# Attention of batch 0 starts once batch 0 is split; batch 1 is split by GpSimd inside the head loop; k and v from a folded weight

## The reference, cut to what matters

```
k, v = x @ Wk, x @ Wv;   q = x @ Wq
latent = (k + v) @ W_down_kv          # 32 features
k_rec, v_rec = latent @ W_up_k, latent @ W_up_v
scores = q . k_rec * scale            # per head, clipped
scores *= exp(-1e-4 * |i - j|)
out = softmax(scores) @ v_rec
```

## Time and profile before

| | us |
|---|---|
| median of 3 runs | 1162.07 (1161.68 to 1163.52) |
| the profiled execution | 1161.56, span 1159.8 |
| first scores of attention | at 91.75 |
| TensorE busy | 1048.4 (90%) |
| VectorE busy | 854.3 (74%) |
| ScalarE busy | 819.0 (71%) |
| GpSimd busy | 226.8 (20%) |

### The profile page before, as it was taken

One profiled execution on the slowest core, in us unless ns is written; L12 is line 12 of the kernel. 1 busy time (PEld: TensorE's weight loads), 2 busy tenths in 40 slices (PEclk: granted clock), 3 DMA queues, 4 the chain that ended last, 5 costly groups with the idle time before them and its releaser, 6 DMA issues.

```text
span 1159.8 us, 20386 instructions
## 1 busy us (share of the span) xinstructions
PE 1048.4 (90%) x5228; PEld 690.5 (60%) x5260; DVE 854.3 (74%) x1998; ACT 819.0 (71%) x1339; POOL 226.8 (20%) x316
## 2 busy tenths in 40 slices
PE   4637999999999659999999999999998998899997
PEld 2212322223222427888888888888885776777876
DVE  5953344433444587999999999999997787688897
ACT  5447999999999346887787788788775443266665
POOL 7553444454445200000000000000004112000000
PEclk9768999999999889999999999999999999699999
DMA  3454666666666217666776766666641000043231
GB/s 98 118 155 147 219 208 196 209 216 214 198 202 210 71 35 292 245 247 231 244 248 232 241 250 232 239 251 233 236 171 55 1 1 1 3 137 120 87 109 37
DMA packets 92918, 192.54 MB, mean 166 GB/s; under 512 B 9676, under 2 KB 56396, under 8 KB 82636
## 3 DMA queue, kind: packets, MB, share of 16 engines
q1 hardware_dynamic: 92884, 192.15, 49.1%
HBM read 154.03 MB, written 38.08 MB: 166 GB/s over the span
## 4 chain that ended last, share of the span: by engine, by line
PE 79%; DVE 9%; issue 4%; ACT 3%; POOL 2%; DMA 2%; ACTq 0%; DVEq 0%; SPq 0%; POOLq 0%
PE bank L1163 25%; PE bank L1176 15%; PE bank L1033 10%; PE bank L1170 8%; PE bank L1015 6%; PE bank L1018 5%; ACT ring L811 2%; PE bank L1265 1%; PE bank L1044 1%; DVE xn L1356 1%; DVE ring L1406 1%; POOL m_norm L722 1%; PE bank L1249 1%; DMA ring<-c_rows 1%; DVE stats L1344 1%
## 5 line engine op out<-in xcount | busy, mean ns | idle before, releaser
L811 ACT ACTIVATE ring<-bank,minus_bound 128x1024 f32<-128x1024 f32 x256 | 271.1, 1110 | 30.5 <-DVE bank L1439 13.6
L1163 PE MATMUL bank<-xh,w_parts 128*128 128x512 f32 x896 | 277.3, 391 | 1.8 <-DVEq L1564 1.8
L867 ACT ACTIVATE bank<-bank 128x512 f32<-128x512 f32 x320 | 186.2, 582 | 91.0 <-PE bank L1163 91.0
L1578 DVE TENSOR_TENSOR bank<-bank,ring 128x512 f32<-128x512 f32 x320 | 223.7, 699 | 29.8 <-DMA ring<-c_rows 6.6
L1176 PE MATMUL bank<-hh,w_parts 128*128 128x512 f32 x776 | 239.8, 390 | 0.0
L1570 DVE TENSOR_TENSOR hl<-bank,hh 128x512 fp32r<-128x512 f32 x321 | 218.2, 680 | 0.1
L1439 DVE TENSOR_TENSOR bank<-bank,corner 128x128 f32<-128x128 f32 x256 | 76.4, 299 | 173.7 <-PE bank L1018 145.1
L861 ACT ACTIVATE hh<-bank 128x512 fp32r<-128x512 f32 x321 | 190.4, 593 | 3.1 <-DVE bank L1578 3.0
L1163 PEld LDWEIGHTS bank<-xh,w_parts 128*128 128x128 f32 x896 | 168.0, 188 | 38.0 <-DVEq L1564 2.3
L1163 PE MATMUL bank<-xl,w_parts 128*128 128x512 f32 x448 | 174.7, 390 | 0.0
L1176 PEld LDWEIGHTS bank<-hh,w_parts 128*128 128x128 f32 x776 | 145.9, 188 | 30.6 <-ACT hh L861 0.4
(11 more groups left out here) (259 smaller groups left out, 1193.0 us busy)
## 6 DMA issues: line engine op xcount, KB each, us to landing
ring<-c_rows SPq DMA_DIRECT2D x80, 1024.0 KB, 5.1
w_parts<-w_pairs SPq DMA_DIRECT2D x160, 128.0 KB, 2.5
w_pairs<-xh SPq DMA_DIRECT2D x16, 768.0 KB, 4.4
q_stack<-q_parts SPq DMA_DIRECT2D x64, 144.0 KB
k_stack<-k_parts SPq DMA_DIRECT2D x64, 144.0 KB
w_pairs<-xl SPq DMA_DIRECT2D x16, 512.0 KB, 3.5
ring<-c_rows SPq DMA_DIRECT2D x16, 512.0 KB, 4.5
big<-in_w_exp SPq DMA_DIRECT2D x16, 384.0 KB, 4.8
```

What stands on the lines that cost most here:

```text
L811: act.activation(ring[:, c % RING * S:(c % RING + 1) * S], wide[c % 2][:], ACT.Exp, bias=minus_bound[:]).then_inc(exp_done, 1)
L867: act.activation(bank(4 + c % ZB), bank(4 + c % ZB), ACT.Silu).then_inc(silu_ready, 1)
L1163: ins = pe.matmul(out_, w[i], x_[j], start=start and k == 0, stop=stop and k == 2, skip_group_check=not start)
L1578: dve.tensor_tensor(bank(4 + c % ZB), bank(4 + c % ZB), cb[u][:, g * GW:(g + 1) * GW], ALU.mult).then_inc(hid_ready, 1)
```

## The change

- k and v come from one folded weight a_up = (Wk + Wv) W_down W_up, made at the start by three small products with a ScalarE copy behind each. TensorE then needs one product of xnT for k and one per tile for v; it forms them between the transposes of later groups. ScalarE's order is written out by hand.
- VectorE and GpSimd split groups 0 and 1 only. Third parts are written by the last subtraction straight as bf16, so a third cast falls away on both. `folded`, `parts` and `qk_f` have a buffer for each group that needs one.
- q is stored as three rows, and loaded threefold; k is stored by one DMA of three parts (384 KB). A group takes 8 DMAs where it took 16. Heads 0 and 1 are loaded behind the stores of group 1.
- Groups 2 and 3 are eight late parts (two variants of q and of k each). GpSimd makes part 0 before the head loop and part i+1 in turn i, by itself, casts included; SyncE stores it at the end of the turn. Seven turns are written out; then SyncE waits for all late stores and the loop goes on.
- The squares of all groups are reduced by VectorE behind its two splits, with three banks instead of two.
- `decay` and `unfold` are computed only in the slow branch; `corner` comes from 128 columns; its reciprocal is taken between bound and flag, and the flag is set before the correction and `minus_bound`.
- VectorE fills the eight stack buffers with zeros at its start. GpSimd zeroes `hh` and `hl` by four copies at the start of the head loop. The fills of `evac[1]` and `ring` are gone; GpSimd's other early fills stand before the first normalisation.

The diff, cut to its core (blank lines left out):

```diff
...
+        parts = [ring[:, u * 3 * S:(u + 1) * 3 * S].bitcast(BF16).rearrange("p (s i t) -> p s i t", s=4, i=3) for u in range(2)]
+        qk_f = [t.rearrange("p (w t) -> p w t", w=2)
+                for t in (ring[:, 6 * S:7 * S], ring[:, 7 * S:8 * S], big[:, 0:S], big[:, S:2 * S])]
+        late_size = 3 * GW // 2
+        late_homes = [(big, 5 * S + k * late_size) for k in range(4)] + [(xnT, k * late_size) for k in range(2)]
+        late_parts = [t[:, at:at + late_size] for t, at in late_homes]
+        late_parts += [xn[:, :, :].rearrange("p t d -> p (t d)")[:, k * late_size:(k + 1) * late_size] for k in range(2)]
+        late_parts = [t.bitcast(BF16).rearrange("p (i t) -> p i t", i=3) for t in late_parts]
...
-        q_dram = [dram(f"q_parts{s}", [NH, 5, HD, S], BF16) for s in range(2)]
-        k_dram = [dram(f"k_parts{s}", [NH, 3, HD, S], BF16) for s in range(2)]
+        q_dram = [dram(f"q_parts{s}", [NH, 3, HD, S], BF16) for s in range(2)]
+        k_dram = [dram(f"k_parts{s}", [NH, HD, 3, S], BF16) for s in range(2)]
...
-            for g in range(G):
-                b, o = g // 2, (g % 2) * GW
-                if g == 2:
-                    sp.wait_ge(parts_saved[0], 16 * 16)
-                    sp.wait_ge(parts_saved[1], 16 * 16)
-                    sp.wait_ge(stacks_zero, 1)
-                    load_stacks(0, 0)
-                    load_stacks(1, 1)
-                sp.wait_ge(parts_ready, g + 1)
-                for w, drams in ((0, q_dram), (2, k_dram)):
-                    if w == 2:
-                        sp.wait_ge(part_cast, 6 * (g + 1))
-                    for v in range(2):
-                        rows = drams[v][b * H:(b + 1) * H]
-                        for i in range(rows.shape[1]):
-                            sp.dma_start(rows[:, i, :, o:o + GW], parts[g % 2][:, w + v, i % 3, :]).then_inc(parts_saved[g % 2], 16)
-            for u in range(2):
-                sp.wait_ge(parts_saved[u], 2 * 16 * 16)
+            def store_part(g, s_, part, saved):
+                at = (q_dram, k_dram)[s_ // 2][s_ % 2][g // 2 * H:(g // 2 + 1) * H, :, :, g % 2 * GW:(g % 2 + 1) * GW]
+                if s_ < 2:
+                    for i in range(3):
+                        sp.dma_start(at[:, i, :, :], part[:, i, :]).then_inc(saved, 16)
+                else:
+                    sp.dma_start(at.rearrange("h d i t -> (h d) i t"), part).then_inc(saved, 16)
+            for g in range(2):
+                for s_ in range(4):
+                    if s_ == 0:
+                        sp.wait_ge(parts_ready, g + 1)
+                    if s_ >= 2:
+                        sp.wait_ge(folded_ready, 6 * g + 4 + s_ - 1)
+                    store_part(g, s_, parts[g][:, s_, :, :], parts_saved)
+            sp.wait_ge(parts_saved, 2 * 8 * 16)
+            sp.wait_ge(stacks_zero, 1)
+            load_stacks(0, 0)
+            load_stacks(1, 1)
+            def store_late(k):
+                sp.wait_ge(late_ready, k + 1)
+                store_part(2 + k // 4, k % 4, late_parts[k], late_saved)
...
-                with sp.Fori(0, NH // 2 - 1) as i:
+                for i in range(7):
+                    next_heads(i, whole)
+                    if i == 0:
+                        store_late(0)
+                    store_late(i + 1)
+                sp.wait_ge(late_saved, 2 * 8 * 16)
+                with sp.Fori(7, NH // 2 - 1) as i:
...
-            for u in range(2):
-                for v in range(2):
-                    link.sign(pool.memset(q_stack[v][u][:], 0.0))
-                    link.sign(pool.memset(k_stack[v][u][:], 0.0))
...
-            link.sign(pool.memset(evac[1][:], 1.0))
-            link.sign(pool.memset(ring[:, 6 * S:8 * S], 0.0))
-            link.wait()
-            pool.sem_inc(stacks_zero, 1)
-            pool.wait_ge(table, 5)
...
+            pool.wait_ge(folds_ready, 1)
+            for g in range(2):
                 pool.wait_ge(k_ready, g + 1)
+                if g:
+                    pool.wait_ge(xnT_ready, G)
                 for w in range(2):
...
+                    pool.tensor_tensor(folded[g][2 + w], qk_f[g][:, 1, :], fold[:, w, g * GW:(g + 1) * GW], ALU.mult).then_inc(folded_ready, 1)
+                for w in range(2):
+                    pool.wait_ge(part_cast, 4 * g + w + 1)
+                    pool.tensor_tensor(folded[g][2 + w], folded[g][2 + w], parts[g][:, 2 + w, 0, :], ALU.subtract)\
+                        .then_inc(folded_ready, 1)
+                for w in range(2):
+                    pool.wait_ge(part_cast, 4 * g + 2 + w + 1)
+                    pool.tensor_tensor(parts[g][:, 2 + w, 2, :], folded[g][2 + w], parts[g][:, 2 + w, 1, :], ALU.subtract)\
+                        .then_inc(folded_ready, 1)
...
+            def late_part(k):
+                g, s_ = 2 + k // 4, k % 4
+                part, cols = late_parts[k], slice(g % 2 * GW, (g % 2 + 1) * GW)
+                if k:
+                    pool.wait_ge(late_ready, k)
+                link(pool.tensor_tensor(late_f, qk_f[g][:, s_ // 2, :], fold[:, s_ % 2, cols], ALU.mult))
+                link(pool.tensor_copy(part[:, 0, :], late_f))
+                link(pool.tensor_tensor(late_f, late_f, part[:, 0, :], ALU.subtract))
+                link(pool.tensor_copy(part[:, 1, :], late_f))
+                pool.tensor_tensor(part[:, 2, :], late_f, part[:, 1, :], ALU.subtract).then_inc(late_ready, 1)
...
+            def begin_heads():
                 link.n = first
                 take_values(0, 0)
                 take_values(1, 1)
+                for t in (hh, hl):
+                    for u in range(2):
+                        link.sign(pool.tensor_copy(t[u][:], across(m_norm[:, 0, 0:1], GW)))
+                link.wait()
+            def two_heads(i, wait_products, late=None):
+                for u in range(2):
+                    split_chunk(i, u)
+                    if late and u == 0:
+                        late_part(late)
+                    wait_products(i, u)
+                    take_values(i * 2 + (2 + u), u)
+            def fast_products(i, u):
+                pool.wait_ge(pv_done, i * (2 * QT) + ((u + 1) * QT + RING))
...
+            with pool.If(fast == 1):
+                begin_heads()
+                late_part(0)
+                for i in range(7):
+                    two_heads(i, fast_products, i + 1)
...
+            take_xnT(0)
+            take_xnT(1)
+            take_qk(0)
+            take_xnT(2)
+            take_qk(1)
+            take_xnT(3)
+            cast(0, 0)
+            take_v(0)
+            take_qk(2)
+            cast(0, 1)
+            take_v(1)
+            take_qk(3)
+            square(0)
+            cast(1, 0)
+            take_v(2)
+            square(1)
+            cast(1, 1)
+            square(2)
+            take_v(3)
+            square(3)
...
+            pe.matmul(bank(7)[:, 0:P], wk[:], ident[:], start=True, stop=False)
+            pe.matmul(bank(7)[:, 0:P], wv[:], ident[:], start=False, stop=True).then_inc(w_up_psum, 1)
+            pe.wait_ge(w_up_ready, 1)
+            pe.matmul(bank(7)[0:LAT, P:2 * P], w_down[:], w_T, start=True, stop=True).then_inc(w_up_psum, 1)
+            pe.wait_ge(w_up_ready, 2)
+            pe.matmul(bank(7)[:, 2 * P:4 * P], a_T, w_up[:], start=True, stop=True).then_inc(w_up_psum, 1)
+            def values_of(g):
                 if g:
                     pe.wait_ge(v_ready, g)
                 for t in range(TPG):
-                    ins = pe.matmul(bank(6)[:, t * P:(t + 1) * P], latT[:, t * P:(t + 1) * P], w_up[:, D:2 * D],
+                    ins = pe.matmul(bank(6)[:, t * P:(t + 1) * P], xnT[:, g * GW + t * P:g * GW + (t + 1) * P], a_up[:, D:2 * D],
                                     start=True, stop=True)
...
-            squares_of(G - 1)
+            def products_of(g):
+                cols = xnT[:, g * GW:(g + 1) * GW]
+                pe.wait_ge(xnT_ready, g + 1)
+                if g == 0:
+                    pe.wait_ge(w_up_ready, 3)
+                if g >= 2:
+                    pe.wait_ge(q_ready, g - 1)
+                    pe.wait_ge(k_ready, g - 1)
+                pe.matmul(bank(2 + g % 2), wq[:], cols, start=True, stop=True).then_inc(q_psum, 1)
+                pe.matmul(bank(4 + g % 2), a_up[:, 0:D], cols, start=True, stop=True).then_inc(k_psum, 1)
+                if g:
+                    values_of(g - 1)
+            def squares_of(g):
+                for w in range(2):
+                    n = 2 * g + w
+                    pe.wait_ge(qk_sq_ready, n + 1)
+                    if n >= 3:
+                        pe.wait_ge(sq_taken, n - 2)
+                    pe.matmul(bank((7, 0, 1)[n % 3])[0:H, :], head_ones[:], qk_sq[g % 2][w], start=True, stop=True).then_inc(sq_psum, 1)
...
-            link(dve.memset(evac[0][:], 0.0))
-            for t in (hh, hl):
-                for u in range(2):
-                    link.sign(dve.tensor_copy(t[u][:], evac[0][:]))
```

(44 more changed lines are left out.)

209 lines of the change are left out of this document (85 added, 124 removed).

## The result

The changed kernel takes 1133.74 us (median of 4 runs, 1132.91 to 1137.73) against 1161.88 (1161.38 to 1163.52) for the kernel before on the same chip: ratio 0.9762, 95% interval 0.9737 to 0.9788. It is faster by 28 us. 1126 had been forecast, with 1118 to 1137 as the range. So sign and range hold, but the forecast's own case (1122 to 1131) does not. The profiled execution took 1134.39 us, span 1132.7.

The account below looks back on a forecast made before the run. Bounds: a 91.75 us stage before the first scores with no engine full, then ScalarE's exponentials. 1161.56 - 37.3 (earlier scores) + 1.5 (loop) = 1125.8; 0.5 added for the median gives 1126.3, say 1126; range 1118 to 1137.

Parts of the forecast that it names:

- the forecast's own case: Whole kernel: scores can start between 51 and 58 us, time 1122 to 1131; chance 0.60.
- Zero fill: Start of the kernel: VectorE's eight fills, priced by elements at 0.97 each, end at 8.7, 1.9 us after x lands.
- by-bytes bound: Start of the kernel: the eight fills priced by bytes, 8 x 0.48 = 3.9 us, end at 4.9, before x lands.
- Splitting batch 0: First stage: VectorE's split of two groups, 10.8 us plus 9.9 for sharing with GpSimd, from 18.9, ends at 39.6.
- Path (b): Split to first scores over squares, reductions, root and flag: 39.6 + 10.3 + 2.3 + 2.3 = 54.5, the later path.
- Path (a): Split to first scores over group 1's stores and head 0's loads: 39.6 + 13.7 = 53.3.
- The loop: Head loop: late parts of 5.1 us fit GpSimd's waits; held closing products cost 1.5 us in all.
- the rival of a slow cast: Head loop: GpSimd's cast to bf16 is slow, GpSimd bounds seven turns; at 6.2 us a cast, time 1173; chance 0.03.
- The contention with the closing products: Head loop: GpSimd's late parts block VectorE's closing products beyond its idle 1.00 us, eight times 0.3, taken as 1.5.
- The loop pays: Head loop: GpSimd holds up the closing products, 10 to 18 us, or queue delays loads; 1134 to 1143; chance 0.15.
- Early start: First stage: cheap fills, squares at full clock, less overlap; scores at 46 to 50, time 1118 to 1122; chance 0.17.
- Head 16 waits for late parts: Head loop at head 16: nothing unless several parts lag, then 5 to 10 us, time 1131 to 1136; chance 0.05.

Follow-up runs that it names:

- experiment 4: The changed kernel with GpSimd's twelve operations on k of batch 0 replaced by fills of zero; one run, 1125.55 us.
- experiment 2: The changed kernel with q and k stored as in the kernel before and both stack loads with 24 rows outermost; 1129.88 us, ratio 0.9718 to before.
- experiment 3: The kernel before with the outer two dimensions of both stack loads exchanged, 3 outermost in place of 24; 1224.85 us, ratio 1.0545.
- Experiment 1: The changed kernel with each k stack loaded by three transfers of 24 rows in place of one with 3 outermost; 1124.54 us, ratio 0.9676 to before.

## Why the prediction was right, and where it was not

**What bounds and where the gain is: right.** The stage before the scores was what could shrink, batch 0 is enough for heads 0 to 15, and what lies behind attention kept its time (779.8 and 780.1 us). The sign and the order of the gain came from that alone.

**Zero fill: wrong by 1.9, on the late side.** The prediction took the fills by elements, 0.97 each. They are 0.485, because the instruction that reached VectorE writes 512 words of four bytes. They ended at 5.25, before x. The by-bytes bound of the prediction is what happened. The Trainium skill (VectorE: DVE Perf Modes, Zero memsets can be issued as uint32 (trn2)) names this form for a fill of zero, and the trace agrees. The last normalisation is 1.35 now that GpSimd fills nothing beside it (2.54 before), as argued.

**Splitting batch 0: the sum right by luck, its terms wrong.** 39.6 forecast, 39.67 measured. The start was 1.8 earlier and the sharing dearer by as much: 11.7 us beyond VectorE's own 10.8, of which experiment 4 puts 10.7 on what GpSimd's operations do more than fills. The prediction's 9.9 came from the rate of one pair of two-tensor operations, 0.42, applied to all of VectorE's work. The casts do worse: beside GpSimd a pair is 2.56 to 2.81 for 0.76, a rate of 0.27 to 0.30.

**Path (b): 54.5 forecast, 52.0 from its rows.** The flag ends at 49.69 where 39.6 + 10.3 + 2.3 = 52.2 had been written. The squares were the mis-sized term. Of the five products taken at 1.78, one took 1.86, two 1.58 (four records in 3.16) and the last two 0.94, 6.9 in all for 8.9, so the reductions ended 8.0 after the split and not 10.3. The small steps took 2.0 for 2.3.

**Path (a): this step failed.** The words were "it lands 2.4 later (the 128 KB row)". It landed 6.91 later. The row was one of a store from 128 partitions, and the transfer is a load whose outermost dimension is three. Of the 4.5 us too little, 1.0 is the row: the same load with 24 outermost lands in 3.44 (experiment 2). 3.5 is the order of the dimensions, and experiment 3 shows that this order alone slows a kernel down. The deeper fault is that the diff's exchange of the two dimensions got no term at all, and no word on what would cover it. The rest of the path was right: stores and landing 8.6 forecast, 39.67 to 47.71 = 8.0 measured; the loads put the last 2.7 behind the first, as forecast (47.73 to 50.39).

**The loop: +1.5 forecast, 7.2 measured, and not for the reason given.** GpSimd's part lasts 5.1 us as forecast (1.26 + 0.61 + 1.15 + 0.61 + 1.15 and the hand-overs; 53.54 to 58.62 for the first), and the cast to bf16 is 0.61 as taken, which ends the rival of a slow cast. The contention with the closing products, the one term of the 1.5, did happen, and cost the loop nothing. Their groups by form before and, in the second fence, after (us busy, mean ns):

```profile
L1464 DVE TENSOR_TENSOR o_heads<-o_sum,o_inv 128x32 f32 x60 | 9.7, 192 | 0.0
```

```profile
L1554 DVE TENSOR_TENSOR o_heads<-o_sum,o_inv 128x32 f32 x60 | 14.5, 273 | 0.0
```

The median is 0.192 as before, but in five of the seven turns one product takes 1.04 to 1.17 us, and in a sixth 0.41. Each of the five lies beside the last subtraction of a late part, as here the second of two products, which ends at 87.82:

```profile
86.51 1.31 DVE L1554 TENSOR_TENSOR o_heads<-o_sum,o_inv 128x32 f32 x2
...
86.61 1.16 POOL L671 TENSOR_TENSOR big<-big 128x512 bf16<-128x512 f32 x1
```

The Trainium skill (SBUF — State Buffer, Who interferes with whom) names this pair, a VectorE instruction with two SBUF inputs against a GpSimd one that reads SBUF, and the trace agrees. But one product a turn is held, not two, and 0.84 to 0.98 beyond its own 0.19 fits into the 1.00 us for which VectorE is idle behind the pair. Experiment 1 has five such products too (1.02 to 1.05 us), and its loop takes 286.5 us against 287.4. Measured, the term is nothing.

**The rivals.** "The loop pays" gave 1134 to 1143; the median is just under its lower edge. Its first half, held products, happened and was free, as shown above. Its second half, a heavier queue that delays a head's load, is half right: the queue was heavier because each k load took twice as long (6.91 for 3.44), not because there were more stores. "Early start" had two of its causes right, the cheap fills and faster squares, and path (b) would have let scores start at 52.0; the load hid it. "Head 16 waits for late parts" was called nothing unless several parts lag. It is the one place where the loop stops (5.2 us), because there a store landing of 7.5 and a load of some 7 follow each other, where the prediction had 4.1 and 2.4.
